# Graph attention on one core: sums stores issued by ScalarE, and earlier loads of the next stage's weights and vectors

## Chip, cores and metric

One core of a Trainium2 chip runs the whole kernel. The metric is device time in microseconds of one execution; the time before is the median of three runs.

## What is computed

A graph attention layer over 625 nodes and 20,000 edges sorted by destination, followed by a mixture of experts. All in float32. What the change touches is the attention and the start of the feed-forward after it:

```python
h = layer_norm(node_feature, ln1_g, ln1_b)
q, k, v = (h @ Wqkv + bqkv) split into three, 8 heads of 64        # q scaled by 512 ** -0.5
a = einsum('ehd,ehd->eh', q[src], k[dst]) + dist_attn + path_attn   # one logit per edge and head
sa = softmax of a over the edges of one destination
agg = segment_sum(v[src] * sa, dst)
h1 = node_feature + agg @ Wo + bo
h2 = gelu(layer_norm(h1, ln2_g, ln2_b) @ W1 + b1) @ W2 + b2
x = x + h1 + h2                    # then the mixture of experts on layernorm(x)
```

## The kernel before

**Sorted edges become dense rows.** The factor exp(dist + path) of each edge is kept as three bf16 parts. For every group of three destination nodes the edges' factors are summed into a dense row over all source columns (628, the node count rounded up), one row per destination and head. A block `w` is four such groups: 128 rows, of which 96 are used. There are 53 blocks. The attention of one head over a tile of 126 destinations (a unit, 40 in all; a pair is the two heads that share a 128-row chunk, so there are 20 pairs, four to a tile) is then exp(q.k) times those sums, normed by its total, turned, and multiplied by v.

**Edge records.** The stage before (`projections`) works out the parts in three rounds (`ROUNDS`: 16, 16 and 10 edge blocks). `store_parts` (L134) stores a round to `window_scratch` in DRAM; round 0 is stored at L444 in that stage, rounds 1 and 2 by SyncE at L886 at the head of the attention stage. A group is fetched from there by `load_groups` (L187, the DMA itself is L193) as 128 edges, 56 bytes to a partition, from a start that `load_starts` (L179, L182) reads from a table into registers. Windows of eight blocks fit into SBUF (`RING`). Blocks with w % 4 >= 2 are loaded by POOL, the others by SyncE. Blocks 0 to 5 are loaded before the barrier (`LOADED` = 6, L447 and L489); `place_at` (L173) gives for block w the later block whose windows are loaded in its turn, so that the first such are block 6 (POOL) and block 8 (SyncE).

**The attention stage, five queues with an order written out by hand.**

- VectorE: `masks`, `products` (group weights, L982) and `onehots` (L990, four to a block) for a block; `guards` (L998, the negative maximum of the logits), `weights` (L1006, exp times sums with the total; L1009, its reciprocal) and `collect` (L1014) for units. It starts with 16 blocks and then takes blocks two ahead of TensorE inside the pairs.
- TensorE: `sums` (L1113, 24 products a block), `logits` (L1123), `turn` (L1135), `weighted_sums` (L1145).
- ScalarE: `copied` (L1061) moves a block's sums from PSUM to one of three buffers `sums_out`, having waited for the store of the block three before; `exps` (L1067), `norm` (L1072), `keep` (L1077).
- SyncE: `block(w)` (L892) loads a later block's windows if w is even, waits for the copy and stores the sums (L901). `unit_rows(u)` (L903) reads the rows of unit u back, 126 rows of 2.5 KB (L911), into one of four buffers; for the first head of a tile it waits until all blocks of the tile have landed (L907), else until the unit three before is summed.
- POOL: windows of its blocks, then it waits for five small vectors and adds the output bias to the residual rows in five operations (L960).

The first 14 blocks (`leading`) come before pair 0; I call this the lead. Then each pair takes two or three blocks (`pair_blocks`), until pair 14; pairs 15 to 19, the tail, have none. W1 (4 MB, four chunks, `load_w1` at L821, DMA L825) is loaded by SyncE after the blocks of pairs 15 to 18 (L926). The five vectors (L929 to L935) follow after the last pair. Each stage ends with a barrier of all engines: L399 before the attention stage, L280 after it. A path for very long segments (`attention_any`) lies behind the opposite branch and isn't taken with these inputs.

The order of SyncE's queue in one block, and of ScalarE's:

```python
if w % 2 == 0 and nxt < WB:                      # SyncE, L895
    load_groups(sp, nxt, starts, rec2_d, windows, g_in)
sp.wait_ge(w_copied, w + 1)
sp.dma_start(sums_d[w, :, :], sums_out[w % 3]).then_inc(out_done[w % 3], 16)

act.wait_ge(w_ready, w + 1)                      # ScalarE, L1059
wait_past(act, out_done[w % 3], 16 * (w // 3))
act.activation(halves(sums_out[w % 3]), psW(w), ACT.Copy).then_inc(w_copied, 1)
```

## Time and profile before

| what | us |
|---|---|
| median of 3 runs (lowest to highest) | 815.55 (814.41 to 818.85) |
| the profiled execution | 812.19 |
| its span, first to last instruction | 810.2 |
| attention stage, between the barriers | 95.6 to 313.6 |
| lead: start to first use of unit 0 | 96.7 to 138.3 |
| pairs with blocks (0 to 14) | 138.3 to 267.0 |
| tail pairs (15 to 19) | 267.0 to 302.9 |
| ScalarE's copy of a block's sums (L1061) | 0.69 |
| VectorE's idle stretches in its 16 leading blocks | 1.29 (for a window), 1.38 and 0.52 (for TensorE) |
| busy over the span: TensorE, VectorE, ScalarE, POOL | 696.5, 532.6, 417.8, 121.8 |

PE is TensorE's matrix products, PEld its weight loads, DVE is VectorE, ACT ScalarE, POOL GpSimd, SP SyncE. A name with q (SPq, POOLq) is the engine's sequencer: DMA issues, drains and semaphore waits. Times are microseconds from the start of the span, unless marked ns. `windows`, `sums_out`, `sums_scratch` are the tiles and DRAM tensors of the kernel. An idle time stands in brackets with what ended it. The granted clock is a share of TensorE's full 2.4 GHz.

### The profile page before, as it was taken

The numbers are of one execution on the slowest core, as the hardware profiler recorded it, in microseconds if no ns is written. First come the engines' busy times: TensorE is split into PE (matmuls) and PEld (weight loads), VectorE is DVE, ScalarE is ACT, GpSimd is POOL, SyncE is SP. The second block draws the span as 40 slices with busy tenths as digits, with TensorE's granted clock in tenths as the row PEclk, the third lists the DMA queues.
The fourth block names the chain that finished last, engine by engine and source line by source line (L and its number), as shares of the span: only waits on it lengthen the run. The fifth ranks groups of instructions, "written<-read, shape, count | busy, mean of one in ns | idle before, by whom it ended". The sixth has DMA issues, their size and how long they took to land. (4 is left out here: it accounts for less than half of the span.)

```text
span 810.2 us, 14580 instructions
## 1 busy us (share of the span) xinstructions
PE 696.5 (86%) x4978; PEld 547.9 (68%) x4978; DVE 532.6 (66%) x1162; ACT 417.8 (52%) x689; POOL 121.8 (15%) x187
## 2 busy tenths in 40 slices
PE   3988755787879765999999999999999999999994
PEld 2654333454546442599999679968889899887793
DVE  6737594897989531644322654358878888888855
ACT  5235332675767651754333643237767666676640
POOL 7341264242420021000000001300000000000022
PEclk9999886898989976999999999999999999999997
DMA  9734395657565764300002040966767677766114
GB/s 250 193 60 92 77 140 140 201 151 215 170 195 188 235 182 145 128 1 1 1 1 79 0 156 26 377 202 218 247 206 226 235 237 241 259 224 230 64 58 152
DMA packets 104156, 125.62 MB, mean 155 GB/s; under 512 B 32402, under 2 KB 70060, under 8 KB 103564
## 3 DMA queue, kind: packets, MB, share of 16 engines
q1 hardware_dynamic: 96955, 115.06, 45.8%
q0 software_dynamic: 5600, 6.54, 3.5%
q10 hardware_dynamic: 1520, 3.01, 1.8%
q8 instruction: 43, 0.70, 0.3%
q14 instruction: 38, 0.30, 0.1%
HBM read 94.91 MB, written 29.67 MB: 154 GB/s over the span
## 5 line engine op out<-in xcount | busy, mean ns | idle before, releaser
L2220 PE MATMUL ps<-xT,w_hi 128*128 128x480 f32 (+7 forms) x512 | 110.5, 338 | 2.2 <-DVE hT L2039 2.2
L2220 PEld LDWEIGHTS ps<-xT,w_hi 128*128 128x128 f32 x512 | 82.1, 189 | 9.4 <-DVE hT L2039 4.0
L2025 DVE TENSOR_TENSOR w_lo<-weights_far,w_hi 128x1024 fp32r<-128x1024 f32 x64 | 78.0, 1219 | 2.5 <-ACT w_hi L2135 2.2
L2222 PEld LDWEIGHTS ps<-xT,w_lo 128*128 128x128 f32 x512 | 73.5, 190 | 1.5
L2222 PE MATMUL ps<-xT,w_lo 128*128 128x240 f32 (+7 forms) x512 | 74.5, 268 | 0.0
L193 POOL DMA_DIRECT2D windows<-window_scratch x104 | 59.7, 577 | 93.0 <-DVE onehot L990 76.2
L1113 PE MATMUL ps<-onehot,group_weights 128*32 128x314 bf16 x1272 | 59.7, 331 | 15.8 <-DVE onehot L990 8.2
L2135 ACT ACTIVATE w_hi<-weights_far 128x1024 fp32r<-128x1024 f32 x64 | 67.1, 1051 | 0.0
L990 DVE TENSOR_SCALAR onehot<-iota_h,windows 128x628 bf16<-128x628 f16 x212 | 66.8, 378 | 0.0
L2245 PE MATMUL ps<-w_hi,hidden 128*128 128x512 f32 (+3 forms) x176 | 62.2, 405 | 2.7 <-DVE hidden L2049 1.9
L1135 PE MATMUL ps<-ident,weights 126*128 126x126 f32 (+1 forms) x200 | 34.0, 308 | 32.2 <-ACT weights L1072 22.6
L1113 PEld LDWEIGHTS ps<-onehot,group_weights 128*32 128x32 bf16 x1272 | 34.6, 109 | 39.3 <-DVE onehot L990 16.1
L1061 ACT ACTIVATE sums_out<-ps 128x628 f32<-128x628 f32 x53 | 36.7, 692 | 41.4 <-DMA sums_scratch<-sums_out 22.6
L1306 DVE TENSOR_TENSOR ff_hidden_lo<-ff_hidden,ff_hidden_hi 128x628 fp32r<-128x628 f32 x16 | 13.0, 814 | 66.1 <-ACT ff_hidden_hi L1390 66.1
L1135 PEld LDWEIGHTS ps<-ident,weights 126*128 126x128 f32 (+1 forms) x200 | 23.7, 154 | 43.4 <-ACT weights L1072 33.2
L1006 DVE CUSTOM_DVE_ANT_0 weights<-sums_in,exponents 126x628 f32<-126x628 f32 x40 | 32.3, 808 | 30.3 <-DMA sums_in<-sums_scratch 30.3
L1072 ACT ACTIVATE weights<-weights,small 126x628 f32<-126x628 f32 x40 | 32.6, 818 | 34.2 <-DVE small L1009 33.9
L2025 DVE TENSOR_TENSOR w_lo<-weights_near,w_hi 128x1024 fp32r<-128x1024 f32 x35 | 42.8, 1222 | 8.1 <-ACT w_hi L2135 8.1
L1387 ACT ACTIVATE ff_hidden<-ps,vs 128x314 f32<-128x314 f32 x32 | 16.6, 522 | 58.7 <-PE ps L1482 58.7
L2011 POOL DMA_INDIRECT weights_far<-slot_results,gate x5 | 5.1, 1011 | 269.0 <-DMA slot_results<-weights_near 267.8
L775 PE MATMUL ps<-hT,weights_near 128*128 128x320 f32 x128 | 38.6, 465 | 1.6 <-ACT hT L667 1.6
L2245 PEld LDWEIGHTS ps<-w_hi,hidden 128*128 128x128 f32 (+3 forms) x176 | 31.9, 181 | 11.1 <-DVE hidden L2049 2.5
(309 smaller groups left out, 1530.4 us busy)
## 6 DMA issues: line engine op xcount, KB each, us to landing
weights_far<-in_L_ffn_w SPq DMA_DIRECT2D x64, 512.0 KB, 5.6
sums_scratch<-sums_out SPq DMA_DIRECT2D x53, 314.0 KB, 3.3
weights_near<-in_L_ffn_w SPq DMA_DIRECT2D x32, 512.0 KB, 3.5
sums_in<-sums_scratch SPq DMA_DIRECT2D x40, 309.1 KB
weights_near<-in_L_gnn_W SPq DMA_DIRECT2D x4, 1024.0 KB, 13.3
weights_near<-in_L_ffn_sw SPq DMA_DIRECT2D x8, 512.0 KB, 5.0
weights_near<-in_L_gnn_Wqkv SPq DMA_DIRECT2D x3, 1024.0 KB, 8.2
weights_ff<-in_L_gnn_W SPq DMA_DIRECT2D x1, 3072.0 KB, 13.0
```

Of the source, the lines that this page charges most:

```text
L193: eng.dma_start(windows[:, w % RING, j, :], frm.rearrange("(p c) -> p c", p=P)).then_inc(g_in[w % RING], 16)
L775: last = pe.matmul(psum[i % 4][:, 0:HALF], wqkv[:, c, m * P:(m + 1) * P], hT[:, c, half * HALF:(half + 1) * HALF], start=c == 0, stop=c == ...
L990: dve.tensor_scalar(onehot[w % 3][:, j, :], iota_h, windows[:, w % RING, j, 1:2], None, ALU.is_equal)\
L1061: act.activation(halves(sums_out[w % 3]), psW(w), ACT.Copy).then_inc(w_copied, 1)
L1072: act.activation(PR[k][0:TILE], PR[k][0:TILE], ACT.Copy, scale=inv[k][0:TILE]).then_inc(p_ready, 1)
L1113: last = pe.matmul(psW(w)[r, a, :], R[w % 3][:, j, :, part], onehot[w % 3][:, j, a * SH:(a + 1) * SH], start=part == 0, stop=part == 2)
L1135: last = pe.transpose(psP[0:n, t, 0:TILE], PR[u % 2][0:TILE, t * P:t * P + n], ident[0:TILE, 0:TILE])
L2025: dve.tensor_tensor(to[1], raw_rest[n] if v == V else raw[u][n], to[0], ALU.subtract)\
L2135: act.activation(to[0], raw_rest[n] if v == V else raw[u][n], ACT.Copy).then_inc(w_hi_ready, 1)
L2220: pe.matmul(both(bank, cap), w[u % 2][0][:, c, cut], xT(r)[:, c, :, :], start=c == 0, stop=False)
L2222: last = pe.matmul(bank[:, 0:cap], w[u % 2][1][:, c, cut], xT(r)[:, c, 0, :], start=False, stop=c == DC - 1)
L2245: last = pe.matmul(psum[4 + blk][0:rows, :], hid_parts[:, v % 2, m, at:at + rows], w2s[u][wp][:, m, :], start=first and i == 0, stop=final ...
```

## The change

ScalarE stores the sums of the 14 leading blocks itself, right after its copy, and SyncE no longer does. Before the barrier only blocks 0 to 3 are loaded, and there SyncE also stores round 1 of the edge parts; blocks 4 and 5, which both are SyncE's, are loaded in the attention stage, after the store of round 2. ScalarE issues the four chunks of W1 at the head of pairs 4, 7, 10 and 13. SyncE issues the five vectors before the blocks of pair 2. The rest is what the untaken path needs for the same.

```diff
@@ -69,7 +69,8 @@
 REL = LONG + 16
 RING = 8
 AHEAD = 6
-LOADED = 6
+LOADED = 4
+W1_AT = (4, 7, 10, 13)
 SPARE_BLOCKS = 3
 ROUND = 16
 ROUNDS = [(b0, min(ROUND, NEB - b0)) for b0 in range(0, NEB, ROUND)]
@@ -173,7 +174,7 @@
 def place_at(w):
 
 
-    return [b for b in range(LOADED, 2 * WB) if by_pool(b)][w // 2], [b for b in range(LOADED, 2 * WB) if not by_pool(b)][w // 2]
+    return [b for b in range(AHEAD, 2 * WB) if by_pool(b)][w // 2], [b for b in range(AHEAD, 2 * WB) if not by_pool(b)][w // 2]
 
 
 def load_starts(nc, engine, w, tab):
...
@@ -448,6 +449,7 @@
                 if not by_pool(w):
                     starts = load_starts(nc, mybir.EngineType.SP, w, tab) if w % 2 == 0 else starts
                     load_groups(sp, w, starts, rec2_d, windows, g_in)
+            store_parts(sp, 1, rec2, rec2_d, lo_ready, windows_stored)
             sp.dma_start(wo[:, :, :], Wo.rearrange("(c p) n -> p c n", p=P)).then_inc(wo_in, 16)
 
         @block.gpsimd
@@ -825,6 +827,17 @@
         eng.dma_start(w1[:, c, :], W1[c * P:(c + 1) * P, :]).then_inc(w1_in, 16)
 
 
+def load_ff_vectors(eng, bo, b2, b1, ln2_g, ln2_b, rows_b, rows_c, ff_vec_in):
+
+    for i, vec in enumerate((bo, b2)):
+        eng.dma_start(rows_b[:, i * D:(i + 1) * D], vec.rearrange("(a n) -> a n", a=1).broadcast_to([P, D]))\
+           .then_inc(ff_vec_in, 16)
+    eng.dma_start(rows_c[0:MC, :], b1.rearrange("(m p) -> m p", p=P)).then_inc(ff_vec_in, 16)
+    for i, vec in enumerate((ln2_g, ln2_b)):
+        eng.dma_start(rows_c[MC + i * DC:MC + (i + 1) * DC, :], vec.rearrange("(m p) -> m p", p=P))\
+           .then_inc(ff_vec_in, 16)
+
+
 def attention(nc, block, sem, W1, bo, b2, b1, ln2_g, ln2_b, rows_d, rows_b, rows_c, rec2, rec2_d, sums_d, xs, w_near, qT, kT, PT, windows, hT,
               vs, iota_n, ident, tab, small, zeros, psum, banks):
 
@@ -883,11 +896,13 @@
 
     @block.sync
     def _(sp):
-        for r in range(1, len(ROUNDS)):
+        for r in range(2, len(ROUNDS)):
             store_parts(sp, r, rec2, rec2_d, lo_ready, windows_stored)
         longest = sp.value_load(tab[0:1, 2 * NB:2 * NB + 1], min_val=-NE, max_val=NE)
         with sp.If(longest < CHUNK + 1):
-            starts = None
+            starts = load_starts(nc, mybir.EngineType.SP, LOADED, tab)
+            for w in range(LOADED, AHEAD):
+                load_groups(sp, w, starts, rec2_d, windows, g_in)
 
             def block(w):
                 nonlocal starts
@@ -897,8 +912,9 @@
                     wait_past(sp, windows_stored, stored_for(nxt))
                     window_free(sp, nxt)
                     load_groups(sp, nxt, starts, rec2_d, windows, g_in)
-                sp.wait_ge(w_copied, w + 1)
-                sp.dma_start(sums_d[w, :, :], sums_out[w % 3]).then_inc(out_done[w % 3], 16)
+                if w >= leading:
+                    sp.wait_ge(w_copied, w + 1)
+                    sp.dma_start(sums_d[w, :, :], sums_out[w % 3]).then_inc(out_done[w % 3], 16)
 
             def unit_rows(u):
                 tile, h = divmod(u, H)
@@ -921,18 +937,11 @@
                     assert blocks_by(q) >= window_blocks((2 * q + 2) // H)
                     unit_rows(2 * q + 2)
                     unit_rows(2 * q + 3)
+                if q == 2:
+                    load_ff_vectors(sp, bo, b2, b1, ln2_g, ln2_b, rows_b, rows_c, ff_vec_in)
                 for w in pair_blocks(q):
                     block(w)
-                if PAIRS - 5 <= q < PAIRS - 1:
-                    load_w1(sp, W1, w_near, [q - PAIRS + 5], w1_in)
         sp.wait_ge(windows_stored, 16 * len(ROUNDS))
-        for i, vec in enumerate((bo, b2)):
-            sp.dma_start(rows_b[:, i * D:(i + 1) * D], vec.rearrange("(a n) -> a n", a=1).broadcast_to([P, D]))\
-              .then_inc(ff_vec_in, 16)
-        sp.dma_start(rows_c[0:MC, :], b1.rearrange("(m p) -> m p", p=P)).then_inc(ff_vec_in, 16)
-        for i, vec in enumerate((ln2_g, ln2_b)):
-            sp.dma_start(rows_c[MC + i * DC:MC + (i + 1) * DC, :], vec.rearrange("(m p) -> m p", p=P))\
-              .then_inc(ff_vec_in, 16)
         sp.wait_ge(rows_zeroed, 16 * len(ZERO_AT))
 
     @block.gpsimd
@@ -1059,6 +1068,9 @@
                 act.wait_ge(w_ready, w + 1)
                 wait_past(act, out_done[w % 3], 16 * (w // 3))
                 act.activation(halves(sums_out[w % 3]), psW(w), ACT.Copy).then_inc(w_copied, 1)
+                if w < leading:
+                    act.wait_ge(w_copied, w + 1)
+                    act.dma_start(sums_d[w, :, :], sums_out[w % 3]).then_inc(out_done[w % 3], 16)
 
             def exps(u):
                 k = u % 2
@@ -1082,6 +1094,8 @@
                     exps(w - 1)
             for q in range(PAIRS):
                 ws = list(pair_blocks(q))
+                if q in W1_AT:
+                    load_w1(act, W1, w_near, [W1_AT.index(q)], w1_in)
                 norm(2 * q)
                 norm(2 * q + 1)
                 keep(2 * q)
...
@@ -2448,6 +2462,7 @@
         longest = sp.value_load(tab[0:1, LONG:LONG + 1], min_val=-NE, max_val=NE)
         with sp.If(longest > CHUNK):
             load_w1(sp, W1, w_near, range(DC), sem("w1_in"))
+            load_ff_vectors(sp, *ff_vectors, sem("ff_vec_in"))
             with sp.Fori(0, NB) as b:
                 for sweep in range(2):
                     with sp.Fori(0, NCH) as c:
```

## Rows read from the trace of the kernel before

**Rows 1.** Stretches: length; PE, PEld, DVE, ACT, POOL busy; clock, DMA share, GB/s.
```profile
96.00:141.00 45.00, 27.08 (x382) 15.44 (x383) 30.50 (x103) 13.15 (x18) 22.99 (x45) 0.73 0.78 156
...
220.00:262.00 42.00, 34.04 (x508) 22.89 (x502) 38.37 (x122) 29.33 (x44) 6.14 (x10) 0.92 0.63 197
262.00:290.00 28.00, 20.05 (x180) 14.21 (x178) 14.83 (x39) 18.43 (x27) 0.00 (x0) 0.88 0.83 239
290.00:314.00 24.00, 8.28 (x66) 5.97 (x64) 4.16 (x12) 6.91 (x10) 6.14 (x5) 0.63 0.27 81
```

**Rows 2.** Waits from 80 to 330 us: us in total, times, longest.
```profile
DVE weights L1006 <- DMA sums_in<-sums_scratch: 30.3, 12, 7.9
ACT sums_out L1061 <- DMA sums_scratch<-sums_out: 22.6, 11, 4.2
```

**Rows 3.** Timeline of SyncE's queue in the lead: start, us, what it issues.
```profile
96.09 4.54 SPq L138 DMA_DIRECT2D window_scratch<-edge_parts  x1
...
105.10 1.91 SPq L193 DMA_DIRECT2D windows<-window_scratch  x4
...
131.34 0.90 SPq L901 DMA_DIRECT2D sums_scratch<-sums_out  x2
133.93 1.88 SPq L911 DMA_DIRECT2D sums_in<-sums_scratch  x2
```

**Rows 4.** SyncE's queue, L901 and L182 (reading starts): ns min/median/max.
```profile
L901 SPq DMA_DIRECT2D sums_scratch<-sums_out x53: 319/430/1224, 107.1 to 265.5; - x53
...
L182 SPq FUSED_REGOPS  x106: 147/147/169, 81.4 to 242.3; - x106
...
L182 SPq TENSOR_LOAD <-tab x14: 520/1039/1474, 80.6 to 240.9; - x14
```

**Rows 5.** VectorE's timeline in the lead: start, us, operation, idle before it.
```profile
96.69 0.60 DVE L966 CAST iota_h<-iota_n 128x628 f16<-128x628 f32 x1 [4.48 <-issue]
...
129.18 1.25 DVE L990 TENSOR_SCALAR onehot<-iota_h,windows 128x628 bf16<-128x628 f16 x4
138.32 0.81 DVE L1006 CUSTOM_DVE_ANT_0 weights<-sums_in,exponents 126x628 f32<-126x628 f32 x1 [7.89 <-DMA sums_in<-sums_scratch]
```

**Rows 6.** DMA issues: count, KB each, median us from issue to landing.
```profile
sums_scratch<-sums_out SPq DMA_DIRECT2D x53, 314.0 KB, 3.3
...
weights_near<-in_L_gnn_W SPq DMA_DIRECT2D x4, 1024.0 KB, 13.3
...
window_scratch<-edge_parts SPq DMA_DIRECT2D x1, 350.0 KB, 13.8
```

**Rows 7.** Waits from 262 to 290 us: us in total, times, longest.
```profile
DVE weights L1006 <- DMA sums_in<-sums_scratch: 10.5, 4, 3.0
```

**Rows 8.** Timeline at the end of the attention stage and the start of the next.
```profile
299.33 6.14 POOL L960 TENSOR_TENSOR xs<-xs,output_biases 128x512 f32<-128x512 f32 x5 [64.65 <-DMA ff_columns<-in_L_gnn_ln_b]
...
313.89 5.18 PE L1447 MATMUL ps<-wo,hT 128*128 128x512 f32 x8
```

**Rows 9.** The barrier that ends the attention stage (L280): drains, ns, start.
```profile
L280 POOLq DRAIN  x1: 13077/13077/13077, 300.3 to 300.3; - x1
...
L280 DVEq DRAIN  x1: 57/57/57, 303.8 to 303.8; - x1
```

**Rows 10.** The barrier before the attention stage (L399): drains, ns, start.
```profile
L399 DVEq DRAIN  x1: 17/17/17, 92.5 to 92.5; - x1
L399 SPq DRAIN  x1: 122/122/122, 95.3 to 95.3; - x1
```

**Rows 11.** VectorE's timeline, start of pairs 15 and 19 (16 to 18: idle 1.91, 2.98, 2.84).
```profile
266.96 0.81 DVE L1006 CUSTOM_DVE_ANT_0 weights<-sums_in,exponents 126x628 f32<-126x628 f32 x1 [2.79 <-DMA sums_in<-sums_scratch]
...
294.24 0.81 DVE L1006 CUSTOM_DVE_ANT_0 weights<-sums_in,exponents 126x628 f32<-126x628 f32 x1 [2.15 <-DMA sums_in<-sums_scratch]
```

**Rows 12.** Lines L570 (VectorE) and L485 (POOL): ns min/median/max.
```profile
L570 DVE TENSOR_TENSOR edge_parts<-records,edge_work x3: 291/292/1674, 53.5 to 72.0; 128x80 f32<-128x80 f32 x2, 128x50 f32<-128x50 f32 x1
...
L485 POOL TENSOR_TENSOR edge_parts<-records,edge_parts x1: 1607/1607/1607, 72.0 to 72.0; 128x640 bf16<-128x640 f32 x1
```

More of the change, by code:

```diff
@@ L282, in program @@
                               zeros, psum, banks)
-                    attention_any(nc, block, sem, rec_d, W1, w_near, qT, kT, PT, hT, vs, iota_n, ident, ones, tab, small, psum, banks)
+                    attention_any(nc, block, sem, rec_d, (bo, b2, b1, ln2_g, ln2_b, rows_b, rows_c), W1, w_near, qT, kT, PT, hT, vs, iota_n, ident, ones, tab, small, psum, banks)
             rows_T = [lasting(moe_rows, f"rows_{part}", [P, DC, NP], F32R) for part in ("hi", "lo")]
@@ L2405, in _, with attention_any @@
             expert(EX, 0, EX // 2, UM)
-def attention_any(nc, block, sem, rec_d, W1, w_near, qT, kT, PT, hT, vs, iota_n, ident, ones, tab, small, psum, banks):
+def attention_any(nc, block, sem, rec_d, ff_vectors, W1, w_near, qT, kT, PT, hT, vs, iota_n, ident, ones, tab, small, psum, banks):
     with ExitStack() as stage:
@@ L2413, in sb @@
             return t[(slice(None),) * len(shape)]
-        attention_chunks(nc, block, sem, rec_d, W1, w_near, qT, kT, PT, hT, vs, iota_n, ident, ones, tab, small, psum, banks,
+        attention_chunks(nc, block, sem, rec_d, ff_vectors, W1, w_near, qT, kT, PT, hT, vs, iota_n, ident, ones, tab, small, psum, banks,
                          sb("any_biases", [P, CT, P]), sb("any_bias_exp", [P, CT, P]),
@@ L2420, in attention_any, with attention_chunks @@
                          sb("any_minus_big", [P, 1]), sb("any_diag", [P, P]), sb("any_zeros", [P, P]))
-def attention_chunks(nc, block, sem, rec_d, W1, w_near, qT, kT, PT, hT, vs, iota_n, ident, ones, tab, small, psum, banks,
+def attention_chunks(nc, block, sem, rec_d, ff_vectors, W1, w_near, qT, kT, PT, hT, vs, iota_n, ident, ones, tab, small, psum, banks,
                      X, R, onehot, keys, L, PR, XM, rec, miss, minus_big, diag, zeros):
```

## Prediction

> **What bounds the kernel now.** I read the busy time by stretches first, then the waits, then the single queues of the attention stage (about 96 to 314 us), which is all that the diff touches. Beyond 314 us nothing changes but the start.
>
> Between 96 and 141 us no engine is full: VectorE works 30.5 of 45 us, TensorE 27.1, ScalarE 13.2 [rows 1]. The waits say why: ScalarE waits 22.6 us in all for a sum buffer whose store has not landed, and VectorE 30.3 us for head rows read back from those stores [rows 2]. SyncE's queue is the cause. It loads two of every four blocks' windows and stores every block's sums, in one order. From its first in-stage window load at 105.10 to the end of its 14th store at 132.24 it goes almost without rest (27.1 us, 1.94 us a block), and unit 0's read is issued at 133.93 only [rows 3]. A store costs it 0.43 us; one reading of starts costs a load of 1.04 us and eight register steps of 0.15, about 2.5 us with their checks [rows 4]. VectorE is done with its 16 blocks long before: 33.8 us after its start, with 3.2 us of waits in it, and then waits 7.89 us for unit 0 [rows 5].
>
> In the middle (141 to 262 us) VectorE is the bound. It works 38.4 of 42 us there; in the tail, 262 to 290 us, only 14.8 of 28 [rows 1]. There W1's four chunks go down SyncE's queue between the head rows, each lands after 13.3 us instead of the 3.3 us of a sums store [rows 6], and VectorE waits 10.5 us [rows 7].
>
> The stage ends with POOL. Its last operation waits 64.65 us for the small vectors, which stand behind the last W1 chunk, then adds five times (6.14 us) [rows 8], and its drain ends at 313.4 us. VectorE drained at 303.8 us [rows 9]. Everybody waits these last ten microseconds.
>
> **The change, part by part** (minus is a gain).
>
> *Stage boundary: -3.0.* Blocks 4 and 5 are no longer loaded before the barrier, the second round's store is. VectorE drains at 92.5 us, SyncE only at 95.3 [rows 10]. SyncE's queue loses eight loads and one reading of starts, its last 4 us; the store needs part sums that VectorE has ready before its own last round, and costs about 0.4 us like the other unhindered ones. So VectorE becomes last and the barrier opens at about 92.6 instead of 95.6. Kept at 3.0; the ends are 1 (if the 1 MB load of Wo behind the store now blocks as the third store did, 4.54 us [rows 3]) and 3.0.
>
> *Lead: -6.0.* ScalarE stores the 14 leading sums itself: 0.43 us on top of a 0.69 us copy (the table above), 1.1 to 1.3 us a block, under VectorE's 1.9 (30.6 us for 16). SyncE loses 14 x 0.43 = 6.0 us, but takes over the loads of blocks 4 and 5. From 92.6: the last round's store, 0.4 to 4.54 us; a value load, 0.7; starts and eight window loads, 3.6 + 3.9; starts again, 2.8. Block 8's load is then issued at 104.1 to 108.2, against 105.10 now. From there 27.1 - 6.0 = 21.1 us for 14 blocks, 17.3 to the last window ahead of unit 0's read, issued at 121.4 to 125.5. The data allow it at about 123.5: VectorE's one-hots of block 10 some 22 us after its start at 93.6 (11 of its 16 blocks), 115.9, TensorE 1.3, copy 0.7, store 0.4 and 3.3 to landing, and about 2 us for windows that come late. I take 124.9. With the 4.4 us that now lie between this read and unit 0's use (133.93 to 138.32 [rows 3, 5]) unit 0 is used at 129.3: 9.0 us sooner, of which the boundary is 3.0. Ends: -4 (late windows) and -7.6.
>
> *Late windows are the new wait.* Blocks 4 and 5 now stand behind both stores, the last of which lands after 13.8 us [rows 6]. They are issued at 97.4 to 105.5; VectorE wants them some 9 and 11 us after its start, at about 102.6 and 104.5. A stall of up to 4 us lies inside the ends above.
>
> *Vectors beside the third pair: +1.* Five issues on SyncE, 2.2 us, ahead of blocks 20 and 21, whose sums gate later units. SyncE still stores these and has little rest there: two head reads, 2.7 stores, 5.3 window loads and a reading of starts make some 8 us of a pair of 8.6 (15 pairs from 138.32 to 266.96). Ends 0 and 2.4.
>
> *W1 beside pairs 4, 7, 10 and 13: +4.* ScalarE's issues (0.55 us each on SyncE) hide in its waits for the reciprocals. The 4 MB now compete with sums stores (three buffers) and head rows in the stretch where VectorE is the bound. The nearest rows are the tail's: four waits beside four chunks, 9.9 us (the 10.5 of rows 7 hold one of before the chunks and leave out the last of [rows 11]). In the middle a head row is asked for about a pair ahead, with some 3 us to spare, and the chunk is in another queue, so I take 1 us a chunk. Ends 0 and 9.9. By the Trainium skill (DMA: Bandwidth & Descriptors, Queues, rings and completion order) an engine serves its queue rows in turn, a packet at a time; a chunk in ScalarE's row would then delay others by its share and not stand ahead of them, which favours the lower end. No row here shows it.
>
> *POOL's adds beside VectorE: +3.* They move to about 225 us, after POOL's last window load, beside a full VectorE. The trace has one such meeting: a VectorE operation with two SBUF inputs that takes 0.29 us took 1.67 us while POOL's two-input operation of 1.61 us ran [rows 12]. Five adds of 1.25 us can so cost VectorE 0 to 6.3 us; not each will meet such an operation, so half.
>
> *Tail: -8.* Without W1 the four waits go. The four intervals from 266.96 to 294.24 [rows 11] are 27.3 us, less 9.9 of waits 17.4; ScalarE's work of 18.4 us in 28 [rows 1], some 4.6 us a pair, is late next and holds them at 4 x 4.8 = 19.2. Ends -4 and -9.9.
>
> *Stage end: -9.5.* POOL is done by about 240 us, so the barrier follows VectorE's drain: 303.9 + 0.3 against 313.7 [rows 9].
>
> *TensorE's clock: -1.0.* It is granted 0.63 in 290 to 314 us [rows 1], and the first eight products of the next stage take 5.18 us after an idle stretch of 11 us [rows 8]. With that stretch gone part of the slow level (1.2 GHz) may go: ends 0 and -1.7.
>
> Sum: -3.0 - 6.0 + 1 + 4 + 3 - 8 - 9.5 - 1.0 = **-19.5 us**. The profiled execution took 812.19 us (span 810.2), so it gives 792.7; the median of the runs, 815.55, is 3.4 above it, and on that footing the forecast is 796.0.
>
> **The rivals.**
> 1. *The middle pays in full.* W1 costs 9.9 and the vectors 2.4: 7.3 more, 803.3. For: VectorE has no room there. Against: DMA engines idle in parts of it.
> 2. *The lead stays.* Late windows eat all 6.0 beyond the boundary: 802. For: one wait of 1.29 us for a window and the 4.54 us issue exist already. Against: SyncE, which set this stretch, loses 6 us.
> 3. *POOL holds VectorE for all of its adds:* +3.3, 799.3. For: the meeting in rows 12. Against: it is only one. The Trainium skill (SBUF — State Buffer, Who interferes with whom) has it as a rule: the port pair of the two is locked for a whole instruction, against a VectorE operation with two SBUF inputs. The one meeting agrees.
> 4. *Nothing in the middle is felt:* W1 and the adds cost nothing, 7 better, 789.
> 5. *Slower.* Each chunk, issued at the head of a pair, delays the sums stores in flight by its own landing: 13.3 - 3.3 = 10 us [rows 6]. With only three sum buffers ScalarE's copy waits, TensorE's bank and VectorE's next block behind it. Four times 10 instead of 4: +16.5, 832. It decides from 5.9 us a chunk (23.5 / 4). Against: in the tail itself the same chunks made waits of under 3 us.
>
> **How the numbers follow.** Forecast 0.42, rival 4 0.17, rival 1 0.13, rival 2 0.11, rival 3 0.10, rivals 1 to 3 together (-2.9, 812.6) 0.04, rival 5 0.03. A measurement here can tell about 0.5% (4.1 us) from no change. All but the last two are faster by more: 0.93; within 0.5% 0.04; slower 0.03. The range reaches past rival 4 to 785 (tail and lead at their good ends) and past rival 1 to 807 (a bit of another on top).
>
> **What would show it.** Right: barrier opening near 92.6; ScalarE's stores in the lead and its waits for landed sums (18 us in the lead) mostly gone; unit 0 used near 129; pairs 4 to 14 longer by a few us in sum; tail pairs of 4.8 us; no gap of 10 us at the stage end. Wrong: VectorE waiting long for windows in the lead, ScalarE waiting 5 us or more for sum buffers after each chunk, VectorE operations of 1.5 us near POOL's adds, or a new last engine at the end.

## The result and the profile after

The changed kernel takes 806.86 us (median of 13 runs, 803.59 to 811.33) against 816.18 (13 runs, 812.43 to 820.14): the ratio is 0.988, 95% interval 0.986 to 0.991. It is faster by 9.3 us, a little under half of the 19.5 forecast, and lies just inside the upper end of the range (807). The ratios below leave out executions in a slower state; the profiled one of e8 (808.65 us against a median of 800.08) was such, so only large differences are read from it.

I cut each profile at the same places: start (VectorE's first operation of the attention stage), lead (to the first use of unit 0), middle (to the first operation of pair 15), tail (to that of pair 19), end (to SyncE's first issue of the next stage), rest. Both kernels were profiled a second time among the experiments (e11, e12), because single profiles of one kernel differ by a microsecond or two a stage.

| us | before | again (e11) | after | again (e12) | mean change | forecast |
|---|---|---|---|---|---|---|
| start | 96.69 | 96.68 | 99.32 | 95.84 | +0.9 | -3.0 |
| lead | 41.63 | 40.52 | 36.26 | 36.59 | -4.7 | -6.0 |
| middle | 128.64 | 130.63 | 139.29 | 138.08 | +9.1 | +8 |
| tail | 27.28 | 27.05 | 22.01 | 23.64 | -4.3 | -8 |
| end | 19.42 | 20.26 | 9.66 | 10.40 | -9.8 | -9.5 |
| rest | 496.54 | 496.26 | 495.06 | 496.75 | -0.5 | -1.0 |
| span | 810.2 | 811.4 | 801.6 | 801.3 | -9.4 | -19.5 |

The profile after, stretches (length; PE, PEld, DVE, ACT, POOL busy; clock, DMA share, GB/s), to be read beside [rows 1]:

```profile
96.00:141.00 45.00, 25.23 (x392) 13.66 (x396) 33.63 (x114) 16.15 (x22) 24.07 (x45) 0.80 0.59 152
...
220.00:262.00 42.00, 31.25 (x440) 21.34 (x439) 39.24 (x105) 24.96 (x37) 14.26 (x19) 0.85 0.60 185
262.00:290.00 28.00, 20.88 (x259) 14.07 (x255) 20.02 (x55) 21.09 (x32) 0.00 (x0) 1.00 0.70 221
```

Waits from 80 to 330 us, as in [rows 2]:

```profile
DVE weights L1015 <- DMA sums_in<-sums_scratch: 17.9, 11, 4.3
...
ACT sums_out L1070 <- DMA sums_scratch<-sums_out: 7.7, 3, 3.1
```

ScalarE's waits for landed stores fell from 22.6 to 7.7 us, none of it in the lead. SyncE's queue there (start, us, what it issues, as [rows 3]; a row's length runs from its first issue to the end of its last) now issues nothing but window loads for 27 us, and unit 0's read is issued 3.5 us sooner, though the stage began 2.6 us later:

```profile
98.28 0.38 SPq L139 DMA_DIRECT2D window_scratch<-edge_parts  x1
103.07 27.27 SPq L194 DMA_DIRECT2D windows<-window_scratch  x32
130.45 2.83 SPq L927 DMA_DIRECT2D sums_in<-sums_scratch  x2
```

The two barriers, as [rows 9] and [rows 10] (ns min/median/max, start). First the one that opens the stage: VectorE drains at 94.7, but POOL's drain, 3.1 us before, takes 9.6 and ends at 98.0. Everybody waits for it.

```profile
L400 POOLq DRAIN  x1: 9612/9612/9612, 88.4 to 88.4; - x1
...
L400 DVEq DRAIN  x1: 17/17/17, 94.7 to 94.7; - x1
```

Then the one that ends it, where POOL (237.6 + 14.2) is long done and VectorE is last:

```profile
L281 POOLq DRAIN  x1: 14170/14170/14170, 237.6 to 237.6; - x1
...
L281 DVEq DRAIN  x1: 58/58/58, 306.2 to 306.2; - x1
```

VectorE's one-hots (ns min/median/max) and POOL's five adds. One one-hot of 0.38 us took 7.24: it started before POOL's first add and ended when the fifth was over.

```profile
L999 DVE TENSOR_SCALAR onehot<-iota_h,windows x212: 365/377/7241, 100.6 to 267.6; 128x628 bf16<-128x628 f16 x106
```
```profile
L969 POOL TENSOR_TENSOR xs<-xs,output_biases x5: 1252/1265/1281, 237.7 to 242.6; 128x512 f32<-128x512 f32 x5
```

The first operations of pairs 17 to 19 in the tail, as [rows 11]: 5.61 us apart, and none of the three waits for a head row. Pairs 15 and 16 still wait for one, 1.50 and 0.73 us.

```profile
285.66 0.81 DVE L1015 CUSTOM_DVE_ANT_0 weights<-sums_in,exponents 126x628 f32<-126x628 f32 x1 [0.67 <-issue]
...
291.27 0.81 DVE L1015 CUSTOM_DVE_ANT_0 weights<-sums_in,exponents 126x628 f32<-126x628 f32 x1 [0.66 <-issue]
...
296.88 0.81 DVE L1015 CUSTOM_DVE_ANT_0 weights<-sums_in,exponents 126x628 f32<-126x628 f32 x1 [0.67 <-issue]
```

What holds them can be followed from the second product of pair 18 (293.63) to that of pair 19 (299.24): reciprocal, then ScalarE's norm, TensorE's turn, ScalarE's copy of it, TensorE's weighted sums and VectorE's collecting copy, each behind the one before (the turn starts when ScalarE, after the norm, has also copied the first head's turn, 295.40 to 296.08):

```profile
294.67 0.82 ACT L1084 ACTIVATE weights<-weights,small 126x628 f32<-126x628 f32 x1 [1.27 <-DVE small L1018]
...
296.18 0.73 PE L1149 MATMUL ps<-ident,weights 126*128 126x126 f32 x5 [0.85 <-ACT weights L1084]
296.94 0.70 ACT L1089 ACTIVATE weights_turned<-ps 128x630 f32<-128x630 f32 x1 [0.19 <-PE ps L1149]
297.69 1.30 PE L1159 MATMUL ps<-weights_turned,vs 128*64 128x126 f32 x20 [0.79 <-ACT weights_turned L1089]
...
299.04 0.29 DVE L1023 COPY hT<-ps 128x126 f32<-128x126 f32 x1 [1.14 <-PE ps L1159]
299.24 0.80 DVE L1015 CUSTOM_DVE_ANT_0 weights<-sums_in,exponents 126x628 f32<-126x628 f32 x1
```

### The profile page after: what moved, and what is told of

It is laid out like the page before. It is cut to its first block and busy times, and to the rows that moved or that the text cites. A ratio compares the mean times of both kernels' runs of the same rounds, so it can differ in the third digit from the quotient of the medians.

```text
span 801.6 us, 14581 instructions
## 1 busy us (share of the span) xinstructions
PE 693.0 (86%) x4978; PEld 544.1 (68%) x4978; DVE 539.8 (67%) x1162; ACT 417.9 (52%) x689; POOL 123.3 (15%) x187
## 5 line engine op out<-in xcount | busy, mean ns | idle before, releaser
L999 DVE TENSOR_SCALAR onehot<-iota_h,windows 128x628 bf16<-128x628 f16 x212 | 73.6, 410 | 0.0
L1127 PEld LDWEIGHTS ps<-onehot,group_weights 128*32 128x32 bf16 x1272 | 32.7, 107 | 38.9 <-DVE onehot L999 21.0
L2170 ACT ACTIVATE hidden<-hT 128x480 fp32r<-128x480 f32 (+7 forms) x32 | 16.4, 512 | 44.3 <-DVE hT L2057 44.3
L2259 PEld LDWEIGHTS ps<-w_hi,hidden 128*128 128x128 f32 (+3 forms) x176 | 31.8, 181 | 11.1 <-DVE hidden L2063 2.5
```

Source lines behind the costliest of these rows:

```text
L999: dve.tensor_scalar(onehot[w % 3][:, j, :], iota_h, windows[:, w % RING, j, 1:2], None, ALU.is_equal)\
L1127: last = pe.matmul(psW(w)[r, a, :], R[w % 3][:, j, :, part], onehot[w % 3][:, j, a * SH:(a + 1) * SH], start=part == 0, stop=part == 2)
L2259: last = pe.matmul(psum[4 + blk][0:rows, :], hid_parts[:, v % 2, m, at:at + rows], w2s[u][wp][:, m, :], start=first and i == 0, stop=final ...
```

## Experiments

All timed results, median us and ratio to the kernel before with its 95% interval:

| run | what | us | ratio |
|---|---|---|---|
| e1 | after, adds at pair 15 | 800.61 | 0.981 (0.977 to 0.985) |
| e2 | after, second store behind the barrier again | 806.21 | 0.989 (0.984 to 0.995) |
| e3 | after, Wo loaded late | 799.32 | 0.981 (0.977 to 0.985) |
| e4 | after, W1 beside pairs 15 to 18 | 804.33 | 0.988 (0.983 to 0.992) |
| e5 | before + ScalarE's lead stores | 810.97 | 0.993 (0.990 to 0.996) |
| e6 | before + W1 beside 4, 7, 10, 13 | 806.20 | 0.984 (0.979 to 0.989) |
| e7 | e3 + adds spread over pairs 13 to 17 | 800.0 | 0.976 (0.972 to 0.981) |
| e8 | e7 + vectors loaded in the stage before | 800.08 | 0.976 (0.972 to 0.979) |
| e9 | e7 + store held until POOL's windows are in | 797.89 | 0.980 (0.977 to 0.984) |
| e10 | e9 + ScalarE stores all sums | 788.67 | 0.967 (0.964 to 0.970) |
| e13 | e10 + SyncE's waits kept | 795.49 | 0.981 (0.976 to 0.985) |
| e14 | before + ScalarE stores all sums | 797.10 | 0.982 (0.978 to 0.985) |

### The stage boundary: e2, e3, e9, e12

```diff
 # e2: back behind the barrier            # e3: Wo to the end of SyncE's attention queue
-            store_parts(sp, 1, ...)       -            sp.dma_start(wo, Wo) ...
-        for r in range(2, len(ROUNDS)):
+        for r in range(1, len(ROUNDS)):
```

> The changed kernel with the second round's store behind the barrier again, as before the change; Wo is then issued at about 88 us, still before the barrier. The changed kernel's barrier opened at 98.2 us because POOL's drain lasted 9.6 us (88.4 to 98.0) against 3.1 before. Theory A (POOL's drain waits until its own window loads are through, and these stand behind the 560 KB store of small pieces): the drain falls to 3 to 4 us, the barrier opens at 92.5 to 95 us by VectorE's drain. Theory B (it is the 1 MB load of Wo): the drain stays at 6 to 10 us. Theory C (the drain is of a length of its own, unrelated to transfers): unchanged 9.6. The two rounds' stores then run later together, and windows of blocks 4 and 5 stand behind both: VectorE waits 2 to 6 us for windows in the lead, so the total is within 2 us of the changed kernel.

> The changed kernel with Wo's load moved behind SyncE's last head row of the attention stage; the second round's store stays before the barrier. Theory A (the store holds POOL's drain): the drain still lasts 6 to 9 us, less only by what Wo took of the engines, and the barrier opens at 95 to 97 us. Theory B (Wo holds it): the drain falls to 3 to 5 us and the barrier opens by VectorE at 92.5 to 95 us. Without Wo's 1 MB in front the last round's store lands sooner and the windows of the lead with it. Total 1 to 4 us under the changed kernel; if Wo then lands too late for the next stage, a wait of a few us at its start.

In e2 Wo alone was issued at 87.9 and POOL's drain still took 6.77 us; in e3 the store alone was issued, and the drain was 3.15. Read singly, that would blame Wo. But e7, whose code up to the barrier is that of e3, has only the store, and 8.15 us. What differs is the order of two things some tenths of a microsecond apart: whether a large transfer is issued before POOL starts its last window load. After, e7 and e3, timeline (start, us, what; `x2` are the stores of rounds 1 and 2, of which the start given is round 1's) and drain:

```profile
87.39 1.65 POOL L194 DMA_DIRECT2D windows<-window_scratch  x3 [0.35 <-issue]
88.42 0.40 SPq L139 DMA_DIRECT2D window_scratch<-edge_parts  x1
```
```profile
87.64 1.65 POOL L194 DMA_DIRECT2D windows<-window_scratch  x3 [0.36 <-issue]
88.30 9.17 SPq L139 DMA_DIRECT2D window_scratch<-edge_parts  x2
...
L400 POOLq DRAIN  x1: 8150/8150/8150, 88.7 to 88.7; - x1
```
```profile
87.72 1.65 POOL L194 DMA_DIRECT2D windows<-window_scratch  x3 [0.35 <-issue]
89.08 7.06 SPq L139 DMA_DIRECT2D window_scratch<-edge_parts  x2
...
L400 POOLq DRAIN  x1: 3152/3152/3152, 88.7 to 88.7; - x1
```

Each group is three loads of 0.55 us, so the last one starts at 88.49, 88.74 and 88.82: after the large transfer in the first two, before it in e3. So I held the store back by a wait (e9), and looked at the unchanged kernel again (e12).

```diff
+            for w in range(LOADED):
+                if by_pool(w):
+                    sp.wait_ge(g_in[w], groups_in(w))
             store_parts(sp, 1, rec2, rec2_d, lo_ready, windows_stored)
```

> As e7 (adds one by one in pairs 13 to 17, Wo loaded late), and before the barrier SyncE waits for the windows of blocks 2 and 3, which POOL loads, before it issues the second round's store. Theory A (a large transfer issued before POOL's last window load starts holds POOL's queue, whatever it is): the store is now issued at 90 to 91 us, POOL's drain takes 3.1 to 3.3 us as before the change (8.2 in e7, 9.6 after), the barrier opens with VectorE's or SyncE's drain, VectorE's first operation of the stage comes 1 to 5 us after that of the kernel before at the same TensorE clock is not expected: it comes at 93 to 97 us, against 98.1 in e7; total 797, some 2 to 4 us below e7 of the same call's footing. Theory B (the store's writes themselves are what POOL's drain waits for, in whatever order): the drain lasts until a us or so behind the store's landing, near 98 to 100 us, and the total is e7's 800 or worse.

> The changed kernel once more, unchanged. If POOL's long drain hangs on whether the store is issued before or after POOL's last window load starts, which are 0.1 to 0.3 us apart, the drain is either 8 to 10 us again or, with the store later, 3.1 to 3.3 us, and the stage starts at 99 or at 93 to 97. The five adds again hold VectorE's one-hots for some 5 to 7 us while they run, so the middle is 137 to 140 us.

e9's drain is 3.15 us, the stage starts at 94.88, SyncE drains at 89.0. e12, the very code of the changed kernel, happened to issue its store at 88.21, behind POOL's last load (started at about 87.5), and has the short drain:

```profile
L400 POOLq DRAIN  x1: 3224/3224/3224, 87.4 to 87.4; - x1
...
L400 DVEq DRAIN  x1: 17/17/17, 94.5 to 94.5; - x1
```

Eleven profiles carry a store or Wo there or hold it back; all follow the order. Five have the long drain (after, e1, e2, e7, e8): the first large transfer was issued 0.1 to 0.5 us before POOL's last load started, and the drain ended 1.0 to 1.4 us behind that transfer's landing. Six have the short one (e3, e4, e9, e10, e12, e13), with the transfer 0.2 to 2.1 us after that start. In the profile of after it was the store alone, landed at 97.0: Wo, issued behind POOL's load, landed at 98.9, later than the drain's end at 98.0. Why the drain waits isn't shown. POOL's drain ended 1.5 us (e2) to 4.7 us (e1) after VectorE's in those that lost the race, and that is the most that the wait can be worth; e9's median doesn't prove it (797.89 against 813.71 for the kernel before beside it, e7 800.0 against 817.31: the ratios' intervals overlap). How often an execution loses the race is not known. The timed runs of e3 are clearly under those of after (0.981 against 0.988, intervals apart), by more than its profile accounts for (span 798.1 against 801.6 and 801.3).

Even with the short drain the start gains just 0.8 us: VectorE's drain, 92.5 in both profiles of before, is at 94.5 to 94.7 in both of after. The change need not be the reason; TensorE's granted clock accounts for it. Up to there before, after and e12 agree within 0.3 us (the first round's store is issued at 73.7 to 74.0; at 74.9 in e6). Stretches of 74 to 88 us in before, in e6 (whose code is there that of the kernel before) and in after, columns as in [rows 1]:

```profile
74.00:88.00 14.00, 10.23 (x38) 4.95 (x36) 13.39 (x21) 7.08 (x8) 3.76 (x8) 1.00 0.38 49
```
```profile
74.00:88.00 14.00, 10.82 (x32) 5.44 (x31) 13.38 (x22) 8.32 (x9) 3.50 (x7) 0.76 0.32 47
```
```profile
74.00:88.00 14.00, 10.82 (x31) 5.38 (x30) 13.38 (x21) 7.40 (x8) 3.25 (x7) 0.76 0.37 48
```

VectorE's drain follows TensorE's last products of the stage. In the five profiles with the full clock in that stretch (before, e4, e7, e8, e11) it starts at 91.6 to 92.6; in the three at 0.88 (e1, e2, e5) at 92.6 to 93.4; in the eight at 0.76 at 93.6 to 95.8. Both kernels have both: with the code of before, e6 and e14 drain at 95.8 and 95.3, only 0.5 and 0.2 us ahead of SyncE. So the 2.8 us in [rows 10] hang on the clock of that one execution; e11 repeats it, the other three with that code don't.

### POOL's adds: e1, e7

```diff
 # e1, ahead of the vectors' wait          # e7, in the loop of adds (with e3's edit)
+            pool.wait_ge(inv_ready, 31)    +                pool.wait_ge(inv_ready, 2 * (13 + t) + 2)
```

> The changed kernel, but POOL waits for the first reciprocal of pair 15 before its five adds of the output bias; everything else as changed. In the changed kernel one one-hot operation of VectorE took 7.24 us instead of 0.38 while POOL's adds ran from 237.7 to 243.8 us, in the stretch where VectorE is the bound. Theory (the adds lock VectorE out for their whole length): no one-hot operation over 0.5 us; the interval between the first operations of pairs 10 and 11 falls from 15.2 us to 9 to 11; the adds now meet the tail, where VectorE has idle time but POOL's and VectorE's operations still meet once, costing 0 to 6 us there; total 1 to 6 us under the changed kernel, the stage end still set by VectorE's drain. Rival (the long operation comes of something else, the W1 chunk issued at 229.8): the long one-hot stays at about 237 us and nothing is gained.

> The changed kernel with Wo loaded behind the last head row, and POOL's five adds one at a time, each after the second reciprocal of pairs 13 to 17, where VectorE goes on with its reductions from PSUM. In the run with all five adds at pair 15 the one-hots were free and three products of pairs 15 and 16 took 1.59, 1.73 and 1.25 us instead of 0.81. Theory (an add holds VectorE only where a VectorE operation meets it): no VectorE operation of these kinds above 1.3 us, no one-hot above 0.9, middle 134 to 136 with W1 in it, tail 22 to 23, barrier before the stage by VectorE's drain, POOL's last drain over before VectorE's; total 1.5 to 4 us under either of the runs with one of the two edits (800.6 and 799.3). Rival (POOL's drain lasts 8 us or more beyond its last add and sets the stage end): stage end 2 to 6 us longer.

In all five profiles that have the adds where the change put them (after, e2, e3, e4, e12) pair 10, beside which they run, takes 15.2 to 15.3 us; in e1 it takes 11.1, in e7 11.4. The longest one-hot of e1 is 496 ns, its middle 135.39, 3.3 below after's mean of 138.7. The tail pays a little: three of VectorE's exp-times-sums products took 1.25 to 1.73 us instead of 0.81 while POOL added, and POOL's five adds took 7.33 us instead of 6.15 (237.68 to 243.83), so there the two took turns. e7: one add per pair, behind VectorE's second reciprocal, costs nothing that shows (longest one-hot 464 ns, products at most 814 ns); its middle is 136.51. In e2 and e3, whose adds and chunks stand as in after, the middle is 140.85 and 139.24; against the mean of all four (139.4) e1 gains 4.0 and e7 2.8. The rows below are e1's products and e7's one-hots.

```profile
L1016 DVE CUSTOM_DVE_ANT_0 weights<-sums_in,exponents x40: 800/811/1725, 137.1 to 299.4; 126x628 f32<-126x628 f32 x40
```
```profile
L1001 DVE TENSOR_SCALAR onehot<-iota_h,windows x212: 365/380/464, 99.4 to 264.6; 128x628 bf16<-128x628 f16 x106
```

### W1 and the vectors: e4, e6, e8

```diff
 # e4                                       # e6, on the kernel before: the chunks as in after
-W1_AT = (4, 7, 10, 13)                     # e8: load_ff_vectors ahead of store_parts(sp, 0, ...)
+W1_AT = (15, 16, 17, 18)
```

> The changed kernel with the four W1 chunks issued by ScalarE at the head of pairs 15 to 18 instead of 4, 7, 10 and 13, so in the tail as before the change but in ScalarE's queue. In the changed kernel the tail's pairs take 5.6 us without any wait for head rows, held by a loop through VectorE's collecting copy and TensorE's weighted sums. Theory (the chunks cost the middle about 1 to 1.5 us each, and the tail has room): the middle from the first use of unit 0 to pair 15 falls from 139.3 us to 133 to 137, the tail keeps 5.6 to 6 us a pair with waits for head rows under 1 us each; total 1 to 5 us under the changed kernel. Rival (transfers compete alike from either queue): waits of 2 to 3 us a pair as before the change, intervals of 6 to 7 us, and the total the same.

> The kernel before with one part of the change: ScalarE issues the four W1 chunks at the head of pairs 4, 7, 10 and 13, SyncE none in the tail. Theory (W1 costs the middle some 3 us and leaves the tail to its loop of 5.6 us a pair): middle 128.6 to 131 to 133, tail 27.3 to 22 to 23, and the vectors, no longer behind a chunk, land earlier: POOL's five adds start before the last pair, but its drain lasts 13 us after them, so the stage end shortens by 3 to 8 us; total 6 to 12 us faster. Rival (the tail as I forecast it, 4.8 us a pair): tail 19.

> As the run with spread adds and the late Wo, and the five vectors issued by SyncE in the stage before, ahead of the first round's store, where SyncE waits about 8 us for the part sums. Theory (the vectors' 2.2 us of issues in pair 2 delayed the stores of blocks 20 and 21 and the head rows behind them, which is why the interval from pair 3 to pair 4 was 10.1 to 10.8 us in five runs against 8.9 before): that interval falls to 9 us, the middle by 1.5 to 2 us, and nothing else changes. Rival (that interval comes of the earlier start of the pairs, not of the vectors): it stays at 10 to 11 us.

e4: middle 136.31, 2.4 below after's mean; tail 28.58, 5.8 above; VectorE's waits for head rows in the tail are 10.7 us (longest 5.4), about the 10.5 of [rows 7] again, though the chunks now stand in ScalarE's queue. e6 gives the mirror image: middle 132.25 against 129.6, tail 21.56 against 27.2. So four chunks cost about 2.5 us in the middle (3.1 against the mean of four) and about 6 in the tail, there from either queue. The middle's figure is hardly above the 1.2 and 2.0 us between two profiles of one kernel. In the middle a chunk lands after 6.7 us (after), where it took 13.3 before [rows 6]. In e6 the vectors, no longer behind a chunk, come sooner too: POOL's drain ends at 307.5 and the stage end takes 13.56 us instead of 19.8. e8: pair 3, whose head rows stand behind the vectors, takes 10.2 us without them, 8.7 to 10.8 in the kernels that load them there and 8.8 to 9.8 in those that keep them at the end: nothing to be seen.

### Where the lead's gain went: e5, e10, e11, e13, e14

e5 is the kernel before with ScalarE's stores in the lead only.

```diff
 # e10 on e9, and e14 on the kernel before: SyncE stores no sums, ScalarE all 53 blocks'
-                    sp.wait_ge(w_copied, w + 1)
-                    sp.dma_start(sums_d[w, :, :], sums_out[w % 3]) ...
 # e13 on e10: the wait alone comes back
+                    sp.wait_ge(w_copied, w + 1)
```

> The kernel before with one part of the change: ScalarE stores the sums of the 14 leading blocks, SyncE does not. Windows, rounds, W1 and vectors stay as they were. Theory (SyncE's order of issues held the lead): the stretch from VectorE's start to the first use of unit 0 falls from 41.6 us to 33 to 36, with nothing of W1 or the vectors changed the rest keeps its lengths (middle 128.6, tail 27.3, end 19.4), total 6 to 8 us faster. Rival (what was gained here is given back in the middle, because the blocks of pairs 0 to 2 then wait for windows or rows): the lead falls as said, but the middle grows by 3 us or more, as it did in the changed kernel with W1 away (136.3 in the run with W1 in the tail, 4.5 of it POOL's adds).

> The kernel before once more, unchanged, for the spread of its stages. If the middle (first use of unit 0 to pair 15) of 128.6 us is a property of the kernel, it comes within 1 us of that, and POOL's drain before the barrier takes 3.1 us again. If the profile of before was merely a lucky one, the middle is 130 to 133 us and the lead 41 to 43.

> As e9, and ScalarE stores the sums of all 53 blocks, not of the 14 leading ones alone, so that SyncE's queue keeps only window loads and head rows. Theory A (the middle is also bound by SyncE's queue, some 8 us a pair of 8.6 to 9.3, which gives back what the lead wins): the middle, pairs 0 to 14, gets 3 to 8 us shorter than e9's, VectorE's waits for head rows fall, and the total is 3 to 6 us lower. Theory B (VectorE and its loop with TensorE bind the middle, SyncE only waits with it): the middle stays within 2 us; ScalarE's extra 0.43 us a block could even lengthen it by 1 to 2 us.

> As e10 (ScalarE stores all sums), but SyncE keeps its 39 waits for ScalarE's copies of blocks 14 to 52 at the places where its stores stood, and issues nothing there. Theory A (the wait at the head of SyncE's queue is what costs: window loads and head rows behind it are issued 1 to 3 us late, 18 us of such waits in e9): the middle is 132 to 135 us, close to e9's 135.1, and the total 795 to 798. Theory B (the issues themselves cost, 39 of 0.43 us, 17 us of SyncE's queue): the middle stays at 125 to 128 us like e10's 125.2 and the total at 788 to 791. A middle between, 128 to 132, gives both a share.

> The kernel before, with ScalarE storing the sums of all 53 blocks and nothing else changed: blocks 4 and 5, the second round's store, W1 and the vectors stay where they were. If SyncE's stores bound the middle of that kernel too: lead 36 to 38 us as in e5, middle 120 to 125 (e10's 125.2 less W1's 3.3, against 128.6 and 130.6), tail and stage end as before (27 and 20), total 800 to 804. If VectorE binds it there: lead 37, middle 128 to 133, total 808 to 811 like e5.

e5's lead is 4 us shorter than before's mean (36.87 against 41.08), its middle 3.4 longer (133.0 against 129.64), at a granted clock of 0.86 where the two profiles of before have 0.92 and 0.90. By the profiles nearly all is given back: spans of 809.9 against 810.2 and 811.4. The timed runs say otherwise: 810.97 against 817.31 us beside it, ratio 0.993 (0.990 to 0.996), so they keep 3 to 8 us. The kernel before itself took medians of 812.5 to 817.3 us beside the different groups of experiments, and 3.4 us from one profile is little against that. How much the middle gives back stays open; that it has a bound of its own, the next runs show.

| us | e9 | e13 | e10 | before (mean) | e14 |
|---|---|---|---|---|---|
| SyncE in blocks 14 to 52 | waits, stores | waits | neither | waits, stores | neither |
| middle | 135.10 | 129.05 | 125.17 | 129.64 | 122.80 |

SyncE's queue is such a bound. In e9 its sum-store entries stand 18.1 us for ScalarE's copies (waits of SyncE's queue in the middle), with window loads and head rows behind them:

```profile
SPq L919 <- ACT sums_out L1075: 18.1, 13, 2.9
```

VectorE's waits for head rows in the middle, behind the first use of unit 0, add up to 15.5 us in e9 and 4.3 in e10, to 9.5 in e11 and to none in e14. That both together cost the kernel some 10 us is shown by timed runs too (e10's ratio 0.967 against e9's 0.980, intervals apart). How they share it is not: of the 9.9 us in the middle the waits at the queue's head carry 3.9 (e13 less e10) and the 39 issues 6.1 (e9 less e13), but by the timed runs e13 (0.981) is no better than e9 (0.980), which puts nearly all on the waits. The whole of e14, one edit to the kernel before, takes 797.1 us: it gains more than the change did. VectorE's work in the middle is the same in e9 (first) and e10 (columns as in [rows 1]):

```profile
131.95:267.05 135.10, 101.09 (x1454) 66.94 (x1454) 113.49 (x357) 87.69 (x129) 37.84 (x61) 0.90 0.70 206
```
```profile
132.27:257.44 125.17, 94.78 (x1454) 62.95 (x1454) 113.83 (x356) 88.90 (x128) 37.69 (x60) 0.97 0.74 223
```

TensorE's granted clock rose with it, 0.90 to 0.97, and its work fell by 6.3 us. In e13, between the two, it was 0.95. Fewer stalls and a higher clock came together, and how much of the 9.9 us is the clock's was not separated.

## Why the prediction was wrong

The direction was right and most mechanisms were there, but two gains were counted that did not come. By its own steps:

- **Stage boundary, -3.0: failed, +0.9.** "SyncE is last, so VectorE becomes last" left out POOL. The step looked at what SyncE's queue loses and costs, and bounded the store and Wo by their issue time on SyncE alone. In the profile of after the store kept POOL's drain open until it had landed (98.0 against VectorE's 94.7). In e12, where it did not, VectorE itself drained 2 us later than before, at a TensorE clock of 0.76 instead of 1.00 just ahead of it. So the other half of the error is that the 2.8 us between VectorE's and SyncE's drains were taken as a property of the kernel; five profiles with that code have 0.2 to 2.8. 3.9 us of the miss.
- **Lead, -6.0: right in mechanism, -4.7.** Windows came late for 0.4 and 1.6 us (after; 3.6 in all in e12), ScalarE's waits went, unit 0 was used 36.4 us after the start against the 35.7 forecast (129.3 - 93.6).
- **Vectors, +1: nothing to be seen** (e8).
- **W1 in the middle, +4: somewhat less,** 2.5 (e4, e6). Rival 1, the middle pays in full, falls. By the Trainium skill (DMA: Bandwidth & Descriptors, Queues, rings and completion order) a DMA engine takes its queue rows in turn, which I took to favour a chunk in ScalarE's row. In the tail no relief shows: 10.7 us of waits from there (e4), 10.5 from SyncE's own. No run has a chunk in SyncE's row in the middle, so the low cost there can't be put down to the row.
- **POOL's adds, +3: the size was right, the way was rival 3's.** VectorE stood through all five adds, for 6.9 us beyond the one-hot's own 0.38. Pair 10 got some 4 us longer; the middle as a whole got 2.2 (e7) to 3.3 (e1) back when they went, 2.8 to 4.0 against the mean of four. The Trainium skill (SBUF — State Buffer, Who interferes with whom) has the port pair locked for a whole instruction; here it stayed with POOL over five in a row. My +3 assumed that some adds would miss VectorE; none did.
- **The middle lacks a term.** W1 (2.5) and the adds (2.7) make 5.2 of the 9.1. The other 3.9 has no term in the sum, and taking in e2 and e3 leaves some 3 as well. e5's middle lost about as much (3.4) with the lead's gain alone, which fits a gain given back, but e5's timed runs keep most of it, so this link is not shown. I had noted that SyncE's work is "some 8 us of a pair of 8.6" and used it only for the vectors, having called VectorE the bound of the middle from its 38.4 of 42 us. The step that failed is that a VectorE busy for 38.4 of 42 us leaves no other bound: e14 shows 7 us in SyncE's stores and their waits alone. That the middle's total (+9.1 for +8) came out near is in part luck, as W1 and the adds took less than their 7 and this took the rest.
- **Tail, -8: half of it, -4.3.** The waits for W1 did go. The step that failed is "ScalarE's work, some 4.6 us a pair, is late next and holds them at 4.8": a busy sum is not the length of a loop. Product, reciprocal, norm, turn, the copy of what was turned, weighted sums and collect follow one another over three engines, and that loop takes 5.61 us a pair, 22.4 for four, against the 19.2 forecast.
- **Stage end, -9.5: right, -9.8.** Its cover, the move of the adds, cost what is written above.
- **Clock, -1.0: not confirmed.** The rest is -0.5 on average, less than two profiles of one kernel differ (1.7). The first eight products of the next stage took 5.18 us before [rows 8] and 5.76 after (6.20 in e11, 6.68 in e12), at 0.62 of the full clock from 303.5 to 312.5 us, so there the slow level was not avoided. In three of the other nine profiles with the short stage end, e1, e3 and e9, it was: the same eight products took 3.70 us there, at the full clock (the row is e3's). So the gain that I had counted exists, but not in every execution.

```profile
303.56 3.70 PE L1461 MATMUL ps<-wo,hT 128*128 128x512 f32 x8
```


The misses are 3.9 (boundary), 1.3 (lead), 1.1 (middle, from parts that partly cancel) and 3.7 (tail), less 0.3 (end), and 0.5 for the clock: 10.2, which but for rounding is the difference of 19.5 and 9.4. Rival 4 did not come about, nor the slower one: a chunk cost 0.6 us, not 5.9. Rival 2 did not either: the lead stayed shorter by 4.7 us.

e10 beats both kernels: 788.67 us, ratio 0.967. And e14, one edit to the kernel before, is already ahead of the change (0.982 against 0.988).

## What to carry to other kernels

Before a large transfer is moved to another place, ask which engine's drain it will then be in flight beside, not just what its issue costs. An in-order queue that issues transfers and also waits for another engine's results can be a bound even where its work and waits seem to fit; here it paid to let the engine that makes the data store it. And when a wait is removed, take the length of the next loop through all its engines, not the busiest engine's share of it. Before a gap between two engines in one profile is counted as a gain, look at the granted clock ahead of it.

## What the hardware showed that I had not expected

- POOL's drain at a barrier took 3.1 to 3.4 us where no large transfer was issued before POOL's last load started, and 6.8 to 9.6 us, until about a microsecond behind that transfer's landing, where one was. In one and the same program the transfer came 0.1 us before that start in one execution (drain 9.6) and 0.7 us after it in another (3.2).
- POOL's drain runs long behind its additions too: 13.1 us before [rows 9], 14.2 after, 8.2 behind the last single add in e7. It costs nothing where POOL is not last.
- Five POOL additions in a row held one VectorE one-hot for all five (7.24 us instead of 0.38), while VectorE's two-input products took turns with them (at most 1.73 us instead of 0.81).
- TensorE's clock moved a barrier by up to 4 us between executions of the same code: VectorE, which waits for TensorE's last products, drained at 91.6 to 92.6 us where the granted clock from 74 to 88 us was 1.00, and at 93.6 to 95.8 where it was 0.76.
